# Two ternary 3x3 convolutions of images 1 to 3 by pairs of output rows, on one Trainium2 core

## The reference, cut to what matters

```python
x = x + deformable_block(group_norm(x))        # conv for offsets, sampling, GroupNorm
v = group_norm(x)                              # 32 groups
q1, q2 = ternary(w1), ternary(w2)              # each weight -1, 0 or 1
out1 = relu(batchnorm(conv3x3(v, q1)))         # statistics over all 4 images
out2 = batchnorm(conv3x3(out1, q2))
x = x + relu(out1 + out2)
```

## Time and profile before

| | before |
|---|---|
| median of 3 runs | 285.18 us |
| profiled execution: span, first to last instruction | 283.7 us |
| profiled execution: own time beside its span | none is given |
| TensorE, VectorE, ScalarE, GpSimd busy | 250.6, 194.2, 168.2, 142.5 us |
| TensorE's mean granted clock (share of full) | 0.971 |
| chain that ended last, by engine | PE 73%, DVE 15%, ACT 7% |

### The profile page before, as it was taken

One profiled execution on the slowest core, in us unless ns is written; L12 is line 12 of the kernel. 1 busy time (PEld: TensorE's weight loads), 2 busy tenths in 40 slices (PEclk: granted clock), 3 DMA queues, 4 the chain that ended last, 5 costly groups with the idle time before them and its releaser, 6 DMA issues.

```text
span 283.7 us, 5555 instructions
## 1 busy us (share of the span) xinstructions
PE 250.6 (88%) x1980; PEld 217.2 (77%) x1980; DVE 194.2 (68%) x445; ACT 168.2 (59%) x362; POOL 142.5 (50%) x198
## 2 busy tenths in 40 slices
PE   2699998999899999989989989999999959999900
PEld 2477667899797899988988979998887737777700
DVE  5689556989888996779977799772373552216193
ACT  2488675989669878868998778860054034330040
POOL 9300899998658689858669965240000000222042
PEclk9999997999999999999999999999999998999985
DMA  7915676544443323323323343100000000000006
GB/s 217 367 48 180 208 257 234 162 138 134 137 139 119 121 63 106 124 99 110 110 75 103 124 122 115 40 0 2 0 0 2 0 0 0 0 3 0 5 37 263
DMA packets 25593, 28.13 MB, mean 99 GB/s; under 512 B 2509, under 2 KB 23613, under 8 KB 25560
## 3 DMA queue, kind: packets, MB, share of 16 engines
q1 hardware_dynamic: 24912, 25.95, 28.0%
q10 hardware_dynamic: 648, 1.76, 1.8%
HBM read 19.87 MB, written 6.78 MB: 94 GB/s over the span
## 4 chain that ended last, share of the span: by engine, by line
PE 73%; DVE 15%; ACT 7%; issue 2%; DMA 1%; SPq 0%
PE PS L809 25%; PE PS L605 7%; PE PS L723 6%; PE PS L676 5%; PE PS L724 5%; PE PS L725 5%; PE PS L705 5%; PE PS L707 4%; PE PS L706 4%; DVE slo L1328 4%; DVE vlo L1339 3%; ACT vhi L986 2%; PE PS L631 2%; ACT shi L974 2%; DMA xs<-in_x 1%
## 5 line engine op out<-in xcount | busy, mean ns | idle before, releaser
L511 POOL TENSOR_TENSOR vt<-rowm,hat 128x1026 f32<-128x1026 f32 x36 | 70.8, 1966 | 26.6 <-PE PS L685 25.2
L1339 DVE TENSOR_TENSOR vlo<-PS,vhi 128x576 fp32r<-128x576 f32 (+2 forms) x88 | 49.9, 589 | 16.7 <-ACT vhi L986 16.3
L986 ACT ACTIVATE vhi<-PS 128x576 fp32r<-128x576 f32 (+2 forms) x88 | 43.8, 523 | 18.8 <-PE PS L707 18.6
L1328 DVE TENSOR_TENSOR slo<-PS,shi 114x512 fp32r<-114x512 f32 (+1 forms) x68 | 43.2, 675 | 6.1 <-ACT shi L974 5.8
L723 PE MATMUL PS<-vhi,wdhi 128*128 128x256 f32 x144 | 43.7, 303 | 1.1 <-ACT xb L993 1.1
L705 PE MATMUL PS<-shi,patch 114*128 114x288 f32 (+1 forms) x136 | 43.4, 319 | 0.9 <-DVE vlo L1339 0.6
L809 PE MATMUL PS<-xhi,q 128*128 128x512 f32 (+1 forms) x144 | 38.9, 417 | 3.4 <-ACT xhi L1056 3.4
L707 PE MATMUL PS<-shi,patch 114*128 114x288 f32 (+1 forms) x136 | 41.0, 301 | 0.0
L706 PE MATMUL PS<-slo,patch 114*128 114x288 f32 (+1 forms) x136 | 40.7, 300 | 0.0
L724 PE MATMUL PS<-vlo,wdhi 128*128 128x256 f32 x144 | 40.5, 281 | 0.0
L725 PE MATMUL PS<-vhi,wdlo 128*128 128x256 f32 x144 | 40.5, 281 | 0.0
(11 more groups left out here) (160 smaller groups left out, 433.1 us busy)
## 6 DMA issues: line engine op xcount, KB each, us to landing
patch<-xt SPq DMA_DIRECT2D x136, 114.0 KB
xt<-xtt SPq DMA_DIRECT2D x4, 1024.0 KB, 6.3
xs<-in_x SPq DMA_DIRECT2D x3, 512.0 KB, 7.8
wraw<-in_L_conv_w SPq DMA_DIRECT2D x2, 576.0 KB, 9.7
out<-xb SPq DMA_DIRECT2D x4, 256.0 KB, 2.6
wd_raw<-in_L_conv_weight ACTq DMA_DIRECT2D x1, 576.0 KB, 7.0
xs<-in_x SPq DMA_DIRECT2D x2, 256.0 KB, 4.0
omr<-omr SPq DMA_DIRECT2D x8, 64.0 KB, 4.3
```

Source lines behind the costliest of these rows:

```text
L511: g.tensor_tensor(vt[:, n % 2, :, :].rearrange("p t (r j) -> p t r j", r=WR), rowm[:, n % 2, :, :].unsqueeze(3).to_broadcast([P, TAPS, WR, ...
L986: last = a.activation(places(vhi), src, ACT.Copy)
L1328: d.tensor_tensor(lo, src, hi, ALU.subtract).then_inc(slo_ok, 1 if pairs(n) == 2 else 3)
L1339: last = d.tensor_tensor(places(vlo), src, places(vhi), ALU.subtract)
```

## The change

Image 0 stays as it was. Images 1 to 3 take another form. For two neighbouring output rows and one column tap, a 3-row kernel (g0, g1, g2) on four input rows (d0 to d3) needs six products; here it needs four: M1 of d1 + d2 with g0 + g1 + g2, M2 of d2 - d1 with g0 - g1 + g2, M0 of d0 - d2 with g0, M3 of d1 - d3 with -g2. The even output row is M0 + (M1 + M2)/2, the odd one M3 + (M1 - M2)/2. Each M is one bank of 16 row pairs by 32 columns, summed over three column taps, head and tail: 4 x 3 x 2 = 24 matmuls an image. `w` counts six such image convolutions, 0 to 2 for `q1` and 3 to 5 for `q2` (`NW` = 3); `POINTS` orders M1, M2 and then M0, M3.

The new steps for one w are: `point_sum` (VectorE, d1 + d2, 512 elements), `point_planes` (GpSimd, d2 - d1 with 512 and the row differences with 960 or 1024), `point_heads` (ScalarE, two of 1024), `point_tails` (VectorE, two of 1024), 24 matmuls, `point_copy` (ScalarE, M1 or M1 and M2 out of PSUM), `point_sums` (M1 + M2 and M1 - M2, 512 each: GpSimd for w = 0 and 1, else VectorE), `point_ends` (VectorE, the output rows, 512 each), and two `conv_stats` on VectorE. GpSimd also makes the summed weights (`point_weights`, four operations of 384 for each convolution) and zeroes borders. GroupNorm of images 1 to 3 is folded into `point_heads` and `point_tails` as a scale, with twice the mean added in the sums. `whole` and `tails` of these images are gone.

Moved: the group sums of the last two images now stand inside conv parts, after a few matmuls; the first convolution's outputs go to `r1` in SBUF and the second's to `xb` and four banks; the final sums of r1 and x1 on GpSimd are whole images (2 instead of 4 halves), two halves of the end go through ScalarE and GpSimd (`f_lin`, `f_sum`), and the order of the output stores is 4, 2, 1, 3, 6, 0, 7, of which ScalarE's queue issues 4 and 6.

The diff, cut to its core:

```diff
+        W_BANKS = [dict(zip((1, 2, 0, 3), m)) for m in ((3, 4, 5, 6), (0, 1, 2, 3), (4, 5, 6, 7),
+                                                       (2, 3, 4, 5), (6, 7, 2, 3), (4, 5, 2, 3))]
+        POOL_SUMS = (0, 1)
...
+        def point_weight(w, p, kx):
+            return (q1, q2)[w // NW][:, kx, :] if p == 0 else qg[w // NW][:, p - 1, kx, :]
+        def pair_rows(m, e):
+            return square(m).rearrange("p (t e) x -> p t e x", e=2)[:, :, e, :]
+        def point_out(w, e):
+            if w < NW:
+                return pair_rows(r1[:, image_of(w), :], e)
+            if w == NW:
+                return pair_rows(xb[:, image_of(w), :], e)
+            m = (6, 4)[w - NW - 1]
+            return pair_rows(PS[:, m:m + 2, :].rearrange("p a x -> p (a x)"), e)
 
...
+            def point_weights(i):
+                pool.wait_ge(q_ok, K * (i + 1))
+                g0, g1_, g2_ = ((q1, q2)[i][:, K * ky:K * ky + K, :].bitcast(F32) for ky in range(K))
+                g.tensor_tensor(qg[i][:, 2, :, :], g0, g2_, ALU.add).then_inc(qg_ok, 1)
+                pool.wait_ge(qg_ok, 4 * i + 1)
+                even = qg[i][:, 2, :, :].bitcast(F32)
+                g.tensor_tensor(qg[i][:, 0, :, :], even, g1_, ALU.add).then_inc(qg_ok, 1)
+                g.tensor_tensor(qg[i][:, 1, :, :], even, g1_, ALU.subtract).then_inc(qg_ok, 1)
+                pool.wait_ge(qg_ok, 4 * i + 3)
+                g.tensor_scalar(qg[i][:, 2, :, :], g2_, -1.0, None, ALU.mult).then_inc(qg_ok, 1)
...
+                if w < NW:
+                    g.tensor_tensor(plane_part(w, 1)[:, W:HW - W], m[:, 0:HW - 2 * W], m[:, 2 * W:HW],
+                                    ALU.subtract).then_inc(wv_pool, 1)
+                else:
+                    g.tensor_tensor(plane_part(w, 1), r1p[:, b, 0:HW], r1p[:, b, 2 * W:ROWS * W], ALU.subtract).then_inc(wv_pool, 1)
+            def point_sums(w):
+                pool.wait_ge(wc_ok, w + 1)
+                if w:
+                    pool.wait_ge(wy_ok, 2 * w)
+                for e, op in enumerate((ALU.add, ALU.subtract)):
+                    g.tensor_tensor(wsum[:, e * BIG:(e + 1) * BIG], wcopy[:, 0:BIG], wcopy[:, BIG:HW], op).then_inc(ws_ok, 1)
             FOLDED = {-1: ((0, 0),), 0: ((0, 1), (0, 2)), 1: ((0, 3),), 2: ((1, 0),), 3: ((1, 1),), 4: ((1, 2), (1, 3))}
...
+            def conv_points(w, sums=()):
+                pe.wait_ge(qg_ok, 4 * (w // NW) + 4)
...
+                done = 0
+                for m, points in enumerate(POINTS):
+                    last_one = m == 1 and w % NW == NW - 1
+                    steps = [(p, part) for p in points for part in range(2)] if last_one else [(p, part) for part in range(2) for p in points]
+                    for p, part in steps:
+                        pe.wait_ge((wh_ok, wl_ok)[part], 2 * w + m + 1)
+                        if part == 0:
+                            bank_free(w, p)
+                        for i, kx in enumerate((1, 0, 2)):
+                            last = t.matmul(PS[:, W_BANKS[w][p], :], point_weight(w, p, kx), point_in(w, part, p, kx),
+                                            start=(part == 0 and i == 0), stop=(part == 1 and i == 2))
+                            done += 1
+                            for at, what, n, b in sums:
+                                if at == done:
+                                    what(n, b)
+                        if part:
+                            last.then_inc(w_mm, 1)
             def convolutions():
...
-                for b in range(B):
-                    for m in range(4):
-                        conv_part(q2, b, m // 2, m % 2, c2_mm)
+                conv_part(q1, 0, 1, c1_mm, ((4, group_square, GN1, B - 2),))
+                pe.wait_ge(y_done, 1)
+                group_mean(GN8, B - 1)
+                conv_part(q1, 1, 0, c1_mm, ((3, group_square, GN8, B - 1),))
+                conv_part(q1, 1, 1, c1_mm)
+                conv_points(0, ((9, group_mean, GN1, B - 1), (14, group_square, GN1, B - 1)))
+                for w in range(1, NW):
+                    conv_points(w)
+                for part in range(2):
+                    for h in range(2):
+                        conv_part(q2, h, part, c2_mm)
+                for w in range(NW, 2 * NW):
+                    conv_points(w)
 
...
+                    act.wait_ge(wv_edge, 2 * w + 2)
+                act.wait_ge(wv_pool, 2 * w + m + 1)
+                if w < NW:
+                    act.wait_ge(gn_ok, order(GN1, image_of(w)) + 1)
+                    a.activation(point_part(w, 0, m), square(plane_part(w, m)), ACT.Identity,
+                                 scale=scale_of(GN1, image_of(w))).then_inc(wh_ok, 1)
+                else:
+                    a.activation(point_part(w, 0, m), square(plane_part(w, m)), ACT.Copy).then_inc(wh_ok, 1)
+            def point_copy(w):
+                act.wait_ge(w_mm, 4 * w + 2)
+                if w:
+                    act.wait_ge(ws_ok, 2 * w)
+                n = 2 if w in POOL_SUMS else 1
+                m = W_BANKS[w][1]
+                a.activation(wcopy[:, 0:n * BIG], PS[:, m:m + n, :].rearrange("p a x -> p (a x)"), ACT.Copy).then_inc(wc_ok, 1)
...
+                    rectify(r1[:, b, :], r1[:, b, :]).then_inc(r1_ok, 1)
+                point_heads(NW, 0)
+                rectify(r1[:, 3, :], r1[:, 3, :]).then_inc(r1_ok, 1)
+                point_heads(NW, 1)
+                for m in range(2):
+                    point_heads(NW + 1, m)
+                point_copy(NW)
+                for m in range(2):
...
+            def point_sum(w):
+                b = image_of(w)
+                m = plane_rows(w)
+                out = square(plane_part(w, 0))[:, 0:H // 2, :]
+                if w:
...
+                        dve.wait_ge(xlo_ok, 3)
+                    mean = nsm[:, GN1, 4, b:b + 1]
+                    twice = nsm[:, GN1, 10, b:b + 1]
+                    edges = square(plane_part(w, 1))
+                    d.tensor_scalar(edges[:, 0, :], square(m)[:, 1, :], mean, -1.0, ALU.add, ALU.mult).then_inc(wv_edge, 1)
+                    d.tensor_scalar(edges[:, H - 1, :], square(m)[:, H - 2, :], mean, None, ALU.add).then_inc(wv_edge, 1)
+                    link(d.tensor_scalar(twice, mean, 2.0, None, ALU.mult))
+                    d.scalar_tensor_tensor(out=out, in0=pair_rows(m, 0), scalar=twice, in1=pair_rows(m, 1),
+                                           op0=ALU.add, op1=ALU.add).then_inc(wv_sum, 1)
+                else:
+                    dve.wait_ge(r1_ok, b + 1)
+                    d.tensor_tensor(out, pair_rows(m, 0), pair_rows(m, 1), ALU.add).then_inc(wv_sum, 1)
+            def point_tails(w, m):
+                dve.wait_ge(wh_ok, 2 * w + m + 1)
+                hi, lo, src = point_part(w, 0, m), point_part(w, 1, m), square(plane_part(w, m))
+                if w < NW:
+                    d.scalar_tensor_tensor(out=lo, in0=src, scalar=scale_of(GN1, image_of(w)), in1=hi,
+                                           op0=ALU.mult, op1=ALU.subtract).then_inc(wl_ok, 1)
+                else:
+                    d.tensor_tensor(lo, src, hi, ALU.subtract).then_inc(wl_ok, 1)
+            def point_sums(w):
+                dve.wait_ge(wc_ok, w + 1)
+                if w:
+                    dve.wait_ge(wy_ok, 2 * w)
+                for e, op in enumerate((ALU.add, ALU.subtract)):
+                    d.tensor_tensor(wsum[:, e * BIG:(e + 1) * BIG], wcopy[:, 0:BIG], PS[:, W_BANKS[w][2], :], op).then_inc(ws_ok, 1)
+            def point_ends(w, e):
+                dve.wait_ge(ws_ok, 2 * w + (2 if w > NW else e + 1))
+                dve.wait_ge(w_mm, 4 * w + 3 + e)
+                d.scalar_tensor_tensor(out=point_out(w, e), in0=square(wsum[:, e * BIG:(e + 1) * BIG]), scalar=0.5,
+                                       in1=square(PS[:, W_BANKS[w][(0, 3)[e]], :]), op0=ALU.mult, op1=ALU.add).then_inc(wy_ok, 1)
             def beside(n):
                 for b in range(B):
...
+                    point_ends(1, e)
+                for h in range(2):
+                    dve.wait_ge(wy_ok, 4)
+                    conv_stats(BN1, 4 + h, chunk(r1, 4 + h))
+                point_sums(2)
+                for e in range(2):
+                    point_ends(2, e)
+                for h in range(2):
+                    dve.wait_ge(wy_ok, 6)
```

359 lines of the change are left out of this document (267 added, 92 removed).

## The result

The changed kernel takes 284.38 us (median of 20 runs, 281.83 to 287.3); the kernel before, run beside it, 286.06 us (20 runs, 284.9 to 290.01). The ratio is 0.9933, with a 95% interval of 0.9913 to 0.9953: **0.7% faster, 1.9 us, where 5.9 us were forecast**. The profiled execution took 283.5 us with a span of 281.5 us.

A forecast was written before the change was run, and what follows sets the result against it. TensorE's matmuls bound the kernel before, VectorE the changed one. Gains 2.8 + 2.9 + 0.6 - 0.35 = 5.95 us took the span from 283.7 to 277.8; with 1.48 above the span, 279.3 us, range 272.5 to 284.5.

The forecast's parts named there:

- The bound and the ceiling: Both convolutions: VectorE becomes the bound in place of TensorE; 72 fewer matmuls give at most 17.2 us.
- First convolution: From y's last normalisation at 202.4 to the first scale near 229.3: a gain of 2.8 us.
- if the cover is thin, it costs up to 1.5 us, at best 0. I take 0.4: Sampling loop: new GpSimd and VectorE work is mostly covered by GpSimd's waits for TensorE, costing 0.4 us.
- the second scale comes at 36.7: Second convolution, counted from the first scale: 36.7 us where it took 39.57 before, a gain of 2.9 us.
- The alternation's end: Second convolution: VectorE's fourth tail, taking turns with GpSimd's operations, ends 21.1 us after the first scale.
- TensorE will idle about 3 us once: Second convolution: TensorE waits before points 0 and 3 of image 2, whose bank waits for VectorE's middle sums.
- VectorE hides it, as it is the bound: Behind TensorE's pauses: if only nine matmuls are slow each time, they cost nothing.
- The end: After the second scale: VectorE 7.05 us against 7.8, gain 0.6; then 4.6 us to the span's end, loss 0.35.
- (a): Rival: the exclusion between VectorE and GpSimd hardly matters, giving 270.7 us; chance 0.10, for anything under 274.
- (b): Rival: GpSimd's alternate rows cost a fifth more, 285.5 us, or a third more, 290; chances 0.10 no change, 0.05 slower.
- (c): Rival: TensorE's clock stays low through the second convolution after its pauses, giving 289 us; chance 0.05.
- (d): Rival: waits on the pair of sums hold TensorE's banks, so nothing shortens; no own chance, included in the spread.

The follow-up runs named there:

- Experiments 2: Changed kernel with GpSimd's two additions of 1024 elements held back until all six tails of the second convolution are done: 280.76 us, ratio 0.9847.
- e3: Changed kernel with GpSimd's two additions held back behind the tails and the second convolution's plane operations made by VectorE: 279.73 us, ratio 0.9791.
- experiment 7: Group sums put back to their former places in the changed kernel, 289.77 us, ratio 1.0104; their new places alone in the kernel before, 287.75 us, ratio 1.0065.
- e4: Changed kernel with 26 extra unread matmuls of 512 columns in TensorE's pause before the second convolution: 283.84 us, ratio 0.9931.
- e7: Changed kernel with the first convolution's group sums put back where the kernel before had them: 289.77 us, ratio 1.0104.
- experiment 6: Changed kernel with twelve matmuls of image 2 in the second convolution made twice, to fill TensorE's pause there: 282.64 us, ratio 0.9875.
- e1: Changed kernel with the first pair image's preparation (planes, input sum, heads, tails) moved to later slots of the sampling loop: 286.78 us, ratio 1.0039.

## Why the prediction was wrong

**The bound and the ceiling were right.** 72 matmuls went, VectorE became the bound of the first convolution and most of the second, and the pieces with two SBUF sources excluded GpSimd's. Experiments 2 and 3 show it: less work of GpSimd beside VectorE's, less time. The Trainium skill's page "SBUF — State Buffer" (section "SBUF: two separate sides") has the loser block for the whole instruction; the 1.64 us for one column agree, which end with GpSimd's operation.

**First convolution, right to 0.1 us in its long part.** From y to the scale 27.02 us, forecast 26.9, with its waits for GpSimd's planes and middle sums. Part of the agreement is luck: the terms that the prediction lists from y to the last statistics add up to 24.1 us, it used 24.5, and 24.55 were measured. The group sums' move, which the prediction counted as a means to an earlier start, is what carries the change: about 4 to 5 us (experiment 7), but only beside the pair form.

**The step "if the cover is thin, it costs up to 1.5 us, at best 0. I take 0.4" failed.** The loop cost 2.1 us, 3.0 to 3.2 in three other traces (e3, e4, e7). I looked at how long GpSimd waits for TensorE in total; the cost came through another pair, since a VectorE operation of one column that starts inside a delayed GpSimd operation waits for its end, and TensorE for it. The exclusion was written down for tails and input sums and not carried to the smallest operations of the norm chain in the loop, though the trace of before has such a pair: 0.86 us for one column, which ends at 175.73 with GpSimd's operation (VectorE, then GpSimd, before the change):

```profile
174.87 0.86 DVE L1214 SCALAR_TENSOR_TENSOR nsm<-nsm 128x1 f32<-128x1 f32 x1
...
173.75 1.97 POOL L511 TENSOR_TENSOR vt<-rowm,hat 128x1026 f32<-128x1026 f32 x1 [1.58 <-PE PS L685]
```

The first group sum behind the loop starts at 197.57, 1.2 us later than forecast (this execution had reached slot 27 0.3 us early); the norms from there took 5.65 us where 6.05 were counted, so 0.8 us were left at y. The 6.05 is itself more than its listed terms, 2.1, 2.1 and 0.9, which make 5.1. A smaller slip: 960 elements on GpSimd took 2.24 us, as the prediction's own slope gives, where it wrote 2.05.

**The step "the second scale comes at 36.7", with its gain of 2.9 us, failed by 2.4 us.** Two terms of it. The alternation's end was put at 21.1 us; it came at 22.1 (252.38, counted from 230.24): GpSimd began 0.24 us later than counted (3.49 us), and the rest, 0.8 us, fits the fixed cost of the hand-overs, which the prediction named and left out; no run measures it by itself. The other, 1.3 us by experiment 6, is TensorE's second pause: it was forecast ("TensorE will idle about 3 us once") and its length was right at 2.76 us, but the matmuls behind it were counted at 0.239 us. In the trace of before, nine matmuls behind a pause of 3.40 us had taken 3.88 us. The prediction allowed for nine slow ones behind each of the two pauses and priced both at nothing, "VectorE hides it, as it is the bound". Behind the first that held (experiment 4). Behind the second nobody hid it: VectorE had caught up, as its idle times of 1.03 and 0.46 us before 265.57 show. It is also the term that an execution can be spared: e1 was.

**The end** took 7.17 us on VectorE for 7.05 (7.2 with GpSimd's additions), and 4.95 from there to the span's end for 4.6. Around the span lay 2.0 us in the profiled execution, not 1.48, and the median of 20 runs is 0.9 above that execution; the kernel before moved alike, from 285.18 to 286.06. With 3.7 us on the span these make the 5.1 us between 279.3 and 284.38. That 284.38 still lies in the range of 272.5 to 284.5, by 0.1 us, is luck: its upper end was set for rivals (b) and (c), not for what happened.

**The rivals.** (a), that the exclusion hardly matters, is out by the tails of 4.92 and 6.77 us, and (b), dearer alternate rows, too: GpSimd's 512 elements on alternate rows took 1.29 us beside VectorE operations that read PSUM (160.21). (c) was right in kind and wrong in extent: it asked whether the clock stays low throughout, and behind the second pause it was low for nine matmuls and part of the next fifteen, which was enough for a fifth of the forecast gain. The first pause was 6.67 us, where nearly 8 were forecast. (d), a wait for TensorE's banks, is that second pause of 2.76 us, which the prediction had counted. Faster, to which the prediction gave 0.79, is what was measured; its size is a third of the forecast.

**Left open:** why some executions lose about 3.1 instead of 2.1 us in the loop (the extra enters at slot 29), why the clock fell behind three pauses of 2.8 to 2.9 us and not behind a fourth, and whether the norm chain behind the loop can be kept clear of GpSimd's weight sums; this was not tried.
